# Eight-core adaLN block: weight-tile loads moved to GpSimd's queue, and one quantisation slot emitted ahead of a transpose

## The reference

```python
mod = (silu(c) @ wmod).reshape(4, 6, 1, 1024)         # sa, ca, ga, sb, cb, gb
h = layernorm(x) * (1 + ca) + sa                       # x: (4, 4096, 1024) float32
k, q, v = h @ Wk.T, h @ Wq.T, h @ Wv.T
alpha = softmax(q @ (k @ Wa.T).T)                      # 4096 x 4096 for each batch element
x = x + ga * (alpha @ (v @ Wb.T))
h = layernorm(x) * (1 + cb) + sb
def fake_quant(w):                                     # one scale for the whole matrix
    s = max(abs(w)) / 127
    return clip(round(w / s), -128, 127) * s
h = gelu(h @ fake_quant(W_fc).T + b_fc + lora_fc(h))   # W_fc: 4096 x 1024
x = x + gb * (h @ fake_quant(W_proj).T + b_proj + lora_proj(h))
```

## Time and profile before

| | us |
|---|---|
| median of 2 runs | 2822.2 (2821.86 to 2822.53) |
| the profiled execution | 2816.16 |
| its span on its slowest core, core 7 | 2814.6 |
| spans of the 8 cores | 2792.5 to 2814.6 |
| TensorE busy in the span | 1692.8 (60%) |
| VectorE busy | 995.0 (35%) |
| ScalarE busy | 755.6 (27%) |
| GpSimd busy | 420.7 (15%) |

### The profile page before, as it was taken

The page is one execution under the profiler, slowest core; times in us unless marked ns, Lnnn a source line. Parts: engine busy times, 40 slices in busy tenths (PEclk is TensorE's granted clock), DMA queues, the critical chain, the costliest instruction groups (busy, mean ns, idle before and its releaser), DMA issues.

```text
span 2814.6 us, 24604 instructions; the slowest of 8 cores (2792.5 to 2814.6 us)
## 1 busy us (share of the span) xinstructions
PE 1692.8 (60%) x7994; PEld 752.8 (27%) x7994; DVE 995.0 (35%) x1745; ACT 755.6 (27%) x1290; POOL 420.7 (15%) x557
## 2 busy tenths in 40 slices
PE   4531413336566566576666567666508959779598
PEld 1210201122222233233333233333303323323233
DVE  3423333334444454445545554555310120200201
ACT  2320101032211322334443443444213032031220
POOL 0001222213333110122221222222100000000000
PEclk9865755667788778787788788878759979889799
DMA  5514243232222221122222222232153122221130
GB/s 145 171 53 125 88 125 109 90 98 70 68 69 66 75 68 34 60 71 83 94 75 69 92 86 71 76 104 75 56 173 94 41 68 82 75 76 59 50 100 30
DMA packets 90838, 233.36 MB, mean 83 GB/s; under 512 B 23860, under 2 KB 23989, under 8 KB 90696
## 3 DMA queue, kind: packets, MB, share of 16 engines
q1 hardware_dynamic: 64440, 160.32, 19.1%
q0 software_dynamic: 26272, 71.47, 7.2%
HBM read 193.85 MB, written 37.88 MB: 82 GB/s over the span
## 4 chain that ended last, share of the span: by engine, by line
PE 41%; DMA 20%; DVE 16%; issue 10%; ACT 8%; POOL 2%; SPq 1%; DVEq 1%; ACTq 0%; POOLq 0%
PE pE L1417 8%; PE pO L1459 8%; DMA amst<-wfc_in 5%; PE pE L1113 5%; PE pO L1211 5%; DMA amst<-wpj_in 4%; PE pE L1138 4%; ACT h_stage L742 3%; DMA q_stg<-q_sc 3%; DMA wm<-wmod_in 3%; DVE amx L634 2%; PE pE L755 2%; ACT h L1381 2%; POOL q_sc L812 1%; PE pE L1425 1%
## 5 line engine op out<-in xcount | busy, mean ns | idle before, releaser
L1417 PE MATMUL pE<-h,wfcst 128*128 128x512 bf16 x1024 | 246.5, 384 | 3.7 <-DVE lora L1397 3.7
L949 POOL TENSOR_TENSOR qt<-qt,qkf 128x1024 f32<-128x1024 f32 x64 | 149.9, 2342 | 612.9 <-ACT qkf L943 606.6
L1459 PE MATMUL pO<-wpj_sb,hid 128*128 128x512 bf16 x1024 | 226.3, 379 | 15.8 <-DVE outb L1475 12.1
L1113 PE MATMUL pE<-ak_fm,q_stg 128*128 128x512 bf16 x512 | 148.0, 460 | 104.9 <-DMA q_stg<-q_sc 104.9
L634 DVE TENSOR_REDUCE amx<-amst 128x1 f32<-128x256 f32 x256 | 106.7, 417 | 175.4 <-DMA amst<-wfc_in 92.9
L1211 PE MATMUL pO<-u_tm,alphaT 128*128 128x512 bf16 x512 | 137.1, 435 | 15.1 <-DVE alphaT L1090 15.1
L755 PE MATMUL pE<-h_stage,wkaT 128*128 128x512 bf16 x512 | 126.6, 414 | 29.9 <-ACT h_stage L742 29.9
L631 POOL DMA_DIRECT2D amst<-wfc_in x128 | 69.1, 540 | 476.5 <-DVE amx L639 314.5
L733 PE MATMUL pT<-idb,xnb 128*128 128x128 bf16 x256 | 32.4, 306 | 175.5 <-DVE xnb L721 175.5
L1432 ACT ACTIVATE hid<-pE,bfc_col 128x512 bf16<-128x512 f32 x128 | 88.0, 687 | 176.3 <-PE pE L1425 176.3
L1459 PEld LDWEIGHTS pO<-wpj_sb,hid 128*128 128x128 bf16 x1024 | 97.7, 98 | 137.9 <-issue 24.5
(11 more groups left out here) (187 smaller groups left out, 2497.2 us busy)
## 6 DMA issues: line engine op xcount, KB each, us to landing
wfcst<-wfcq_sc SPq DMA_DIRECT2D x128, 256.0 KB, 2.6
wm<-wmod_in SPq DMA_DIRECT2D x32, 768.0 KB, 4.4
x_st<-x_in SPq DMA_DIRECT2D x48, 512.0 KB, 3.9
amst<-wfc_in POOLq DMA_DIRECT2D x128, 128.0 KB, 2.6
amst<-wpj_in POOLq DMA_DIRECT2D x128, 128.0 KB, 2.5
wst<-wfc_in SPq DMA_DIRECT2D x32, 512.0 KB, 3.9
wst<-wpj_in SPq DMA_DIRECT2D x32, 512.0 KB, 4.0
wfcq_sc<-qbf POOLq DMA_DIRECT2D x32, 256.0 KB, 2.3
```

The lines of the kernel that those rows point to most:

```text
L949: t_dd = em("gpsimd", lambda e, qt=qt, qkf=qkf: e.tensor_tensor(out=qt[:], in0=qt[:], in1=qkf[:], op=OP.subtract), waits=[("s", t_kf)], in ...
L1113: t_eA = em("tensor", lambda e, oc=oc, jb=jb, p=p: e.matmul(out=s.pE[:, jb * 512:(jb + 1) * 512], lhsT=s.q_stage[p][:, oc * 128:(oc + 1) * ...
L1417: t_mm = em("tensor", lambda e, ic=ic, oc=oc, p=p, sl=sl: e.matmul(out=s.pE[:, sl * 512:(sl + 1) * 512], lhsT=wfcst[p][:, ic * 128:(ic + 1 ...
L1459: t_mm = em("tensor", lambda e, tt=tt, vc=vc, hc=hc: e.matmul(out=s.pO[:, vc * 512:(vc + 1) * 512], lhsT=hid[:, hc * 512 + tt * 128:hc * 5 ...
```

## The change

Two things are edited. The loads of the weight tiles (lines 923 and 929) are issued by GpSimd instead of SyncE, with the same waits, at the same point of the emission. And slot 4 is emitted before the transposes of half A instead of after them. A third hunk adds an empty line.

```diff
@@ quant_stageA
         if idx == 0:
             src_ap, _, _ = self._qsrc(0)
-            st["dws"][0] = em("sync", lambda e, src_ap=src_ap: e.dma_start(
+            st["dws"][0] = em("gpsimd", lambda e, src_ap=src_ap: e.dma_start(
                 out=s.wstb[0][:], in_=src_ap),
                 waits=[("v", self.t_qfin)], inc="d_ws0")
         if idx + 1 < 64:
             src_ap, _, _ = self._qsrc(idx + 1)
             pn = (idx + 1) % 2
-            st["dws"][pn] = em("sync", lambda e, src_ap=src_ap, pn=pn: e.dma_start(
+            st["dws"][pn] = em("gpsimd", lambda e, src_ap=src_ap, pn=pn: e.dma_start(
                 out=s.wstb[pn][:], in_=src_ap),
                 waits=[("v", st["e1_%d" % pn]), ("v", self.t_qfin)],
                 inc="d_ws%d" % pn)
@@ ph5, at the end of the pass
             if ic > 0:
                 self._emit_pv(ic - 1, st, emit_trans, part=1)
+            pump1()
             tA, evA = emit_trans(0, ic, s.alphaA, t_rs, "v")
             st["transA_done"] = tA
-            pump1()
```

## The result

| | before | after |
|---|---|---|
| median of the runs made side by side, us | 2830.0 (42 runs) | 2837.1 (43 runs) |
| the profiled execution | 2816.16 | 2835.99 |
| its span on its slowest core | 2814.6 (core 7) | 2834.4 (core 5) |
| TensorE, VectorE, ScalarE, GpSimd busy, us | 1692.8, 995.0, 755.6, 420.7 | 1704.2, 996.6, 756.0, 456.9 |

The account below looks back on a forecast made before the run. No engine is full; an engine-to-engine chain in the attention stage sets the pass. +5.3 (new wait for old), -6 (clock), +3.9 (end), +0.3 (first load) = +3.5 us, giving a median of 2825.5, range 2808 to 2848.

Parts of the forecast that it names:

- the likeliest case: Whole kernel: time stays within 2% (56 us) of before, chance 0.91.
- The q wait goes, and another takes its place: TensorE before logits A: 104.9 us of q waits vanish, replaced by a wait for half A's copies behind slot 4.
- The ends meet, +0.35 us: Start of logits A: the new wait ends 0.35 us later than the old in each of 15 passes, +5 us.
- The clock, -0.4 us: Logits A on TensorE: part of the slow-clock stretch falls on the transposes, 0.4 us less a pass, -6 us.
- The loads on GpSimd cost nothing: Weight-tile loads issued by GpSimd: nothing added in the loop, under 1 us once for the first tile.
- the +0.3: First weight-tile load, for which VectorE has to wait: +0.3 us once in the sum.
- The end, +3.9 us: After the last pass: half A's two copies stand between slot 4 and half B's copies, +3.9 us, uncovered.
- the q load of the next tile goes out a whole pass earlier: SyncE's list without weight-tile loads: q leaves early, landing by 1558.4 at the latest; alone removes TensorE's 7.3 us wait.
- The rival that everything vanishes: TensorE before logits A: the stall goes unreplaced, gaining up to 110 us, a time of 2716; chance 0.03.
- The late loads on GpSimd: Line 933 in slot 1: VectorE waits for late tiles; an 18 us landing costs 60 us; chance 0.06 with everything else over 2% slower.

Follow-up runs that it names:

- e3: The changed kernel with each q load also waiting for slot 4's addition of line 973, so it leaves later: 2828.94 us, ratio 1.0020.
- the repeat: The changed kernel measured again, nothing altered: 2839.62 us, ratio 1.0042 to before.
- e1: Against the kernel before, only the weight-tile loads moved to GpSimd, slot 4 staying behind the transposes of half A: 2817.56 us, ratio 0.9977.
- e7: Kernel before with weight-tile loads on GpSimd, line 991 waiting only for its own buffer's store, tiles stored one slot earlier: 2818.38 us, ratio 0.9961.
- e6b: Same as e7, but slot 1 emitted behind the first part of the previous tile's output instead of before the maximum of A: 2676.04 us, ratio 0.9493.

## Why the prediction was right, and where it was lucky

The measured median of 2837.1 us lies in the range of 2808 to 2848, and the time is within 2% of before, as the likeliest case had it: +9.9 us where +3.5 was said. By its steps:

- *The q wait goes, and another takes its place.* Right. From 104.9 us to nothing, and 115.2 us more in the two waits before the transposes. The forecast's signs are all there in the pass shown: 9.16 us before the second group (about 9 was said), 4.29 before line 1018 (about 4), 2.44 us of VectorE before line 973 (2.4), GpSimd's issues at a median of 0.55 to 0.56 us.
- *The ends meet, +0.35 us.* Right in kind, somewhat short. Without the meeting (e3), the logits start 7.29 us behind line 973, where it was 6.70 in the mean of before: +0.6. VectorE's idle time doesn't cover it, since it waits there for TensorE: the maximum of A starts 0.46 us later.
- *The clock, -0.4 us.* Right in the sum, by luck. In e3 the logits A, where the forecast had it, take 9.05 us against 9.16 before (mean of eight cores): 0.11 less, a quarter of the term. The output matmuls of line 1211, which the forecast didn't look at, take 8.44 against 8.85, at a mean granted clock of 0.83 instead of 0.80. Together they give back 0.52, so that of the later start the pass keeps 0.05.
- *The loads on GpSimd cost nothing.* Right for GpSimd's own list and for the tiles: line 933 waits once, for the first tile, 5.3 us against 5.2 before, so of the +0.3 at most 0.1 is there. Wrong as a whole, below.
- *The end, +3.9 us.* Right to the tenth. After, the copies of half A and half B behind the last pass stand at 2016.04, 2017.98, 2019.94 and 2021.89, and the output matmuls follow at 2022.73. The first copy of half B comes 2019.94 - 2016.04 = 3.9 us later than it would in the old order.

**The step that failed** is in edit 1: "the q load of the next tile goes out a whole pass earlier", or "even if it went out only when the second of them is done". I asked only whether the load would land in time, and it does. What I didn't ask is what it meets when it leaves. By my own rows it had to leave with the residual load at about 1552.3, one microsecond before slot 3's store of 1553.31, and line 991 waits for every store issued so far (the semaphore `d_pc0` in its code; neither my account of a slot nor the forecast names that wait). This term was missing from the sum. The slot grew by 0.41 us and the pass by 0.77 (in the repeat 0.24 and 0.59), against 0.05 in e3 without the meeting; so it is 0.5 to 0.7 us a pass, 8 to 11 us. The slot is only half of it: against e3 it is 0.39 us longer, and the output matmuls are 0.38 us longer (8.82 against 8.44), at a granted clock of 0.80 again. Why the meeting cost less in the repeat stays open. With it the sum would be the forecast's +3.5 and 8 to 11 more, 11.5 to 14.5 us; measured were 9.9 (5.4 to 14.4) and, in the repeat, 11.9 (6.5 to 17.3). Without it (e3), +5.7 us (-1.4 to 12.7) were measured for +3.5 forecast.

**The rival that everything vanishes** was priced at up to 110 us, as if TensorE's idle time were the path. e1 and e7 show the price was wrong by its own mechanism: with the logits starting 7 us earlier, edit 1 gains 6.5 us, or 1.06 us a pass with freed stores. The kind of cap was in the rows shown. VectorE idles 3.15 us in front of the copy of 1572.56, and the maximum of A stands behind that; an earlier start of the logits alone can gain no more than this idle time. Its size was not in that one row: in the mean of all passes it is 1.79 us, 27 us in 15. The forecast had read the row, but only as a reserve for a later end, not as the cap for an earlier one. Being right with 0.91 was in this sense cheap: even the whole cap is under half of the 56 us that 2% are.

**The late loads on GpSimd** (0.06) didn't come: landings of 4.2 us in the median and 6.0 at most on core 5 (6.5 over all cores) against a cover of 10.8. The rule of the Trainium skill, "SBUF — State Buffer", section "SBUF: two separate sides", that GpSimd can't write the descriptors of its DMAs while VectorE runs an operation in a two-port mode, had stood against this edit. Little of it shows here: 464 of the 512 loads of the eight cores were issued beside line 978 alone, like that of 1568.30 (line 978 ran from 1567.84 to 1569.07), and their issues lasted 0.53 to 0.56 us. One load on each core was issued beside lines 933 and 940, and lasted 0.76 us. That is 0.2 us once, and no run here shows which of these operations run in such a mode.

## What to carry to other kernels

A load that was held back by chance may be what keeps another transfer clear: when a wait goes, list what its DMAs now leave beside, and who waits for those, not only whether they land in time. A long wait of the busiest engine says how long it stands, not what it is worth; the idle time of the engine behind it, up to the point where the two meet again, is the cap (here 1.8 us a pass, not 7.0), and it is to be taken as a mean over the passes: the one pass that was read in detail had 3.15. And where filler work is spread over a loop, its place in the list of the engine that the main chain needs decides: one slot moved behind the maximum took the pass from 53.58 us (e7) to 46.13 (e6b), where both edits of the change together gave nothing.

## What the runs showed of the hardware

- GpSimd starts to issue a DMA later than SyncE does: 0.57 us after the end of the VectorE operation that it waited for (58 of 62 loads on every core of the kernel after; the pass shown has 1568.30 - 1567.73), where SyncE took 0.07 us in the median of before (0.06 in the pass of the earlier trace rows: 1556.03, with line 973 ending at 1555.97). Hidden here.
- Two loads of together 768 KB, issued 0.5 to 1 us ahead of a store of 256 KB, make the store land 1.2 to 1.9 us later in the median (W_proj 4.09 us against 2.88, W_fc 4.26 against 2.32), and after 6.4 us at most; one of 512 KB alone makes it 0.4 to 0.8 us (W_proj 3.30 and 3.65 against 2.88). The residual store, issued 0.5 us behind that one, went from 3.6 us to 5.0 in the median. Whether the engines that move the data or the memory is what they share stays open. In the stretch of the meeting the DMA engines are busy for 0.76 of the time, and move 250 GB/s:

```profile
1565.50:1573.60 8.10, 0.00 (x0) 0.00 (x0) 5.17 (x7) 4.45 (x5) 1.61 (x4) 0.50 0.76 250
```

- Idle time of TensorE costs where it ends, and moving it moves the cost: with 9 us idle before the transposes of half B (e7) the output matmuls took 9.97 us instead of 8.75 in the pass shown, at a granted clock of 0.50 until 1618, and 9.22 instead of 8.75 in the mean of cores 2 to 7.
